# Where the silu's table is loaded, and five instructions or groups that change places in a decoder block kernel

## The reference, cut to what matters

```python
x = x + mamba2(layernorm(x), ...)       # state space layer, 128 heads of 64, 8 groups, state 128
x = x + cross_attention(layernorm(x), ctx, ctx, mask)   # 32 query heads, 8 key/value heads of 16
x = x + lora_experts(layernorm(x), A, B, Wr)            # 4 experts of rank 16, the best 2 by logits
```

```python
xBC = silu(conv4(proj_xBC) + conv_b)
dt = softplus(proj_dt + dt_bias)
y = ssd(x, A, B, C, D, dt)              # exp of differences of cumulated dt * A
g = y * silu(gate)
out = (g * rsqrt(mean(g * g, group) + eps) * norm_w) @ out_w.T
```

## Time and profile before

| what | us |
|---|---|
| median of 3 runs (3003.57 to 3009.27) | 3006.18 |
| the profiled execution's own time | 3005.64 |
| its span, first to last instruction | 3003.8 |
| PE busy (95% of the span) | 2865.4 |
| DVE busy (69%) | 2059.7 |
| ACT busy (48%) | 1437.4 |
| POOL busy (43%) | 1277.4 |
| ACT table loads, 183 of 1.28 us | 234.8 |

### The profile page before, as it was taken

How to read it: one execution, slowest core, us unless ns; L and a number is a source line. 1 busy time by engine, 2 the same in 40 slices (tenths; PEclk the granted TensorE clock), 3 DMA queues, 4 the chain that set the end, 5 groups by cost and what they waited for, 6 DMA issues and landing times.

```text
span 3003.8 us, 56158 instructions
## 1 busy us (share of the span) xinstructions
PE 2865.4 (95%) x22224; PEld 2294.5 (76%) x22224; DVE 2059.7 (69%) x3144; ACT 1437.4 (48%) x2077; POOL 1277.4 (43%) x820
## 2 busy tenths in 40 slices
PE   5899999999999999999999999999999999999986
PEld 3677777777878778787787878777787887878764
DVE  5677766777766767677676776777666676766656
ACT  3555556555444544444444454444444444444422
POOL 3566665666343343434334333424333342433332
PEclk8999999999999999999999999999999999999996
DMA  5777777777656655555655655555665555565510
GB/s 179 245 261 251 251 255 241 271 247 241 219 185 191 191 172 178 186 176 184 195 186 180 199 180 175 183 184 175 186 196 182 179 182 187 176 195 178 181 57 18
DMA packets 179266, 578.25 MB, mean 193 GB/s; under 512 B 25216, under 2 KB 31872, under 8 KB 170816
## 3 DMA queue, kind: packets, MB, share of 16 engines
q1 hardware_dynamic: 179008, 574.66, 58.5%
HBM read 460.29 MB, written 114.29 MB: 191 GB/s over the span
## 4 chain that ended last, share of the span: by engine, by line
PE 79%; DVE 13%; ACT 4%; issue 3%; DMA 0%; POOL 0%; DVEq 0%; ACTq 0%; SPq 0%; POOLq 0%
PE p_in L429 45%; PE p_out L429 21%; PE p_y L429 8%; PE p_in L508 4%; DVE cv L1148 3%; DVE o_ring L1092 2%; DVE t_y L1184 1%; ACT cv L775 1%; DVE decay L1167 1%; PE p_y L608 1%; DVE decay L1161 1%; ACT decay L775 1%; ACT L775 1%; ACT w_ring L775 0%; DVE x_tok L1172 0%
## 5 line engine op out<-in xcount | busy, mean ns | idle before, releaser
L429 PE MATMUL p_in<-xnb,w_ring 128*128 128x512 f32 x6912 | 1710.2, 400 | 24.1 <-DVE cv L1148 20.0
L429 PEld LDWEIGHTS p_in<-xnb,w_ring 128*128 128x128 f32 x6912 | 1281.3, 190 | 299.4 <-issue 24.1
L1148 DVE SCALAR_TENSOR_TENSOR cv<-p_in,cpar,cv 128x504 f32<-128x504 f32 (+2 forms) x960 | 704.5, 734 | 541.3 <-ACT cv L775 517.5
L1480 POOL TENSOR_TENSOR g_lo<-g_f,g_hi 128x512 fp32r<-128x512 f32 x256 | 332.1, 1297 | 1357.6 <-ACT g_hi L775 1357.6
L429 PE MATMUL p_out<-o_ring,g_hi 128*128 128x512 f32 x2048 | 648.8, 398 | 1.5 <-POOL g_lo L1480 1.5
L775 ACT ACTIVATE cv<-p_in,cpar 128x512 f32<-128x512 f32 x320 | 248.0, 775 | 703.5 <-PE p_in L429 622.5
L429 PEld LDWEIGHTS p_out<-o_ring,g_hi 128*128 128x128 f32 x2048 | 379.3, 188 | 89.7 <-issue 1.9
L429 PE MATMUL p_out<-o_ring,g_lo 128*128 128x512 f32 x1024 | 404.5, 395 | 0.0
L1172 DVE TENSOR_TENSOR x_tok<-p_in,dts 128x512 f32<-128x512 f32 x256 | 176.5, 689 | 289.1 <-PE p_in L508 288.0
L1491 POOL TENSOR_TENSOR ss<-ss,g_sq 128x512 f32<-128x512 f32 x192 | 309.6, 1612 | 7.5
L775 ACT ACTIVATE x_t<-cv 128x512 f32<-128x512 f32 x256 | 160.7, 628 | 302.1 <-DVE t_y L1184 287.0
(11 more groups left out here) (233 smaller groups left out, 2261.2 us busy)
## 6 DMA issues: line engine op xcount, KB each, us to landing
w_ring<-ws_scr SPq DMA_DIRECT2D x432, 512.0 KB, 3.6
o_ring<-ows_scr SPq DMA_DIRECT2D x192, 512.0 KB, 5.3
ws_scr<-w_ring SPq DMA_DIRECT2D x144, 512.0 KB, 4.9
decay<-cum_scr SPq DMA_DIRECT2D x128, 512.0 KB, 6.6
raw_w<-wt SPq DMA_DIRECT2D x144, 256.0 KB, 4.1
ows_scr<-o_ring SPq DMA_DIRECT2D x64, 512.0 KB, 6.2
raw_o<-owt SPq DMA_DIRECT2D x64, 256.5 KB, 5.7
acb<-x SPq DMA_DIRECT2D x3, 1024.0 KB, 6.4
```

The source lines that it names most:

```text
L429: return nc.tensor.matmul(o, lhsT=l, rhs=r, start=first, stop=last)
L1148: ins = V.scalar_tensor_tensor(acc[:, :, t:SEQ], src[:, :, 0:SEQ - t], cpar[:, 5 * m + 3 - t:5 * m + 4 - t], acc[:, :, t:SEQ], ALU.mult, A ...
L1480: T(g_lo[:, c % 2, :], g_f[:, c % 2, :], g_hi[:, c % 2, :].bitcast(F32), ALU.subtract).then_inc(glo_done, 1)
```

## The change

ScalarE gets a silu of one column into a spare tile, called at the start of each pass and at those steps that follow an exp, always directly behind `tap0`. On DVE `experts` moves from `early` to `late`, behind `scored`; the parts of the softplus get other steps; and `refill_o` of step 3 moves behind `late`. On GpSimd `deviation` moves behind `differences` of step 1 (and so behind `shifted`).

```diff
@@ scalar
+            def silu_table():
+                copy(spare[:, :], half_neg[:, 0:1], ACT.Silu)
@@
                 tap0(0, n)
+                silu_table()
                 silu(0, n)
@@
                 for k in range(1, CPG):
                     tap0(2 + k, n)
+                    if (k == 2 and (closing(tb, g) is not None or not begun)) or k == 3 or (k == 4 and is_at(tb, g, 4)) \
+                            or (k == 5 and former(opening(tb, g)) is not None):
+                        silu_table()
@@ vector, early
-                if k == 5 and former(t) is not None:
-                    experts(t - 1, S)
@@ vector, late
                 if k in (5, 6) and t is not None:
                     scored(t, S, k - 5, (y0, y1))
+                if k == 5 and former(t) is not None:
+                    experts(t - 1, S)
                 if k == 6 and u is not None:
                     attended(u, S, y0)
-                if is_at(tb, g, 4) and k in (6, 7):
-                    softplus(tb + 1, {6: (0,), 7: (1, 2)}[k])
-                if is_at(tb, g, 5) and k in (3, 6, 7):
-                    softplus(tb + 1, {3: (3,), 6: (4, 5), 7: (6, 7, 8, 9)}[k])
-                if is_at(tb, g, 6) and k in (3, 6, 7):
-                    softplus(tb + 1, {3: (10, 11), 6: (12,), 7: (13,)}[k])
+                if is_at(tb, g, 4) and k in (4, 7):
+                    softplus(tb + 1, {4: (0,), 7: (1,)}[k])
+                if is_at(tb, g, 5) and k in (3, 4, 6, 7):
+                    softplus(tb + 1, {3: (2,), 4: (3,), 6: (4, 5), 7: (6, 7)}[k])
+                if is_at(tb, g, 6) and k in (3, 4, 6, 7):
+                    softplus(tb + 1, {3: (8, 9), 4: (10,), 6: (11,), 7: (12, 13)}[k])
@@ vector, body
                     x_tokens(k, n)
-                    refill_o(k)
+                    if k != 3:
+                        refill_o(k)
@@
                     late(k, tb, g)
+                    if k == 3:
+                        refill_o(k)
@@ gpsimd, body
-                if coming(tb, g) is not None:
-                    deviation(coming(tb, g))
                 if u is not None:
                     shifted(u, S)
                 for k in range(1, CPG):
@@
                         differences(tb, g, 1, n)
+                        if coming(tb, g) is not None:
+                            deviation(coming(tb, g))
```

More of the change, by code:

```diff
@@ L113, in decoder_kernel @@
         rstd = sb("rstd", [P, 1])
+        spare = sb("spare", [P, 1])
         wd = sb("wd", [P, 2, KT, P], F32R)
```

## The result

The changed kernel takes 2981.55 us (median of 4 runs, 2979.32 to 2982.28), the kernel before 3007.43 beside it: ratio 0.9914, 95% interval 0.9897 to 0.9932. It was forecast at 2980.0 with a range of 2971 to 2994. The profiled execution took 2982.17 us with a span of 2980.4; before, 3005.64 and 3003.8. The total is 1.5 us off. Its parts are further off: two terms were wrong by 2 to 7 us each, in opposite directions.

The account below looks back on a forecast made before the run. TensorE bounds the kernel, so only ending its waits pays. Terms 13.5 + 0.3 + 7.4 + 3.3 + 4.4 + 0.5 - 3.0 - 0.4 = 26.0 us, taking the median 3006.2 to 2980; range 2971 to 2994.

Parts of the forecast that it names:

- The bound: Whole kernel: TensorE has the most work, so an edit pays only where it ends a TensorE wait, no more than that.
- The silu's table: Step 2 of odd passes, blocks 1 to 3: table load runs in ScalarE's idle 3.17 us, 13.5 us gained.
- Rival 2: Table load doesn't move, because the silu lands behind the wait or the load stays: 13.5 us less gain, 2994, chance 0.05.
- The output halves: Block 0, passes 0 to 3, step 3: low half begins earlier, head products' waits of 7.6 us go, 7.4 taken.
- The expert gates: Step 5 of passes 4 and 6: gates moved behind the scores end four waits, 4.1 us, 3.3 after 0.8 back.
- The softplus: Parts respread in blocks 0 to 2: block 0 gains 4.4 us; blocks 1 and 2 lose 0 to 1 each.
- Part 3 at step 4 of pass 5: Softplus part moved there in block 0 runs beside GpSimd's sums and costs perhaps 0.3 us.
- The deviation: Subtraction put ahead of it on GpSimd: costs 3.0 us in block 0's passes 1 to 3, 0.4 in blocks 1 and 2.
- both cases: Block 0, passes 1 to 3: `normal` ends 0.35 us later if first at the port, 1.3 if blocked for a `w_low`.
- The first pass: Subtractions start about 3 us earlier; TensorE's wait for the first decay matrix shrinks 0 to 1.9 us, 0.5 taken.
- Rival 4: Slower: `normal` is late by the whole subtraction, 3.69 us, in all passes: 3013, chance 0.04.
- Rivals 1 and 3: 1: block 0 gives its gains back, 2993, chance 0.14. 3: waits go whole and the deviation costs nothing, 2973, chance 0.09.

Follow-up runs that it names:

- the two runs: One-column silus alone on the kernel before: 2986.73 us, 18.9 less; changed kernel without the silus: 2999.05 us, 17.5 above the changed kernel.
- the old spread of the softplus: Changed kernel with the softplus parts at their old steps: 2982.24 us, ratio 0.9921; also with deviation behind the subtraction only in the first pass: 2976.39 us, 0.9897.
- two pairs: Changed kernel against two kernels with softplus at its old steps: one otherwise unchanged, 2982.24 us; one with deviation also ahead again except in the first pass, 2976.39 us.
- the hold: Changed kernel, with GpSimd in passes 1 to 3 of block 0 waiting until normal is done before its next w_low: 2978.25 us (one run).
- a second 91: Changed kernel with two one-column silus at each of the 91 places: 2981.41 us, ratio 0.9915.

## Why the prediction was right in sum, by its own steps

- **The bound.** Right: what paid was each wait of TensorE. Blocks 1 to 3 follow the sites to a tenth of a microsecond.
- **The silu's table.** The mechanism was right and the term, 13.5, too small: 15.3 us in the 12 odd passes (1.28 each by the 11 periods), 1.3 in pass 4 of blocks 1 and 2, 17.5 to 18.9 us in all by the two runs (block 0's dips and the tail in them). The step that failed is "Ten of the waits are 1.09 us and go whole": they do go whole, but it read the gain off the wait shown, 1.09, instead of the load removed from the chain, 1.28. No extra cost from 91 silus, as said. Rival 2 (the load doesn't move) is refuted by the load's place. On the drain the Trainium skill ("ScalarE: Activation LUTs", "What ACT_TABLE_LOAD costs") has about 2.66 us for each switch; by it the two waits of 1.65 us would have gone whole. They keep 0.37, so 1.28 us went, the load alone, and the one-column silu starts 0.01 us behind the load. No drain is seen here.
- **The output halves.** Right: 7.6 to 0.3 us of waits, 7.4 forecast; by periods up to 10, with clock dips in them.
- **The expert gates.** The wait of 4.1 us went, but not all of it by this edit alone: 1.2 us go with the silu at step 4 as well, and in pass 6 the edit is worth 3.1 us with the old spread of the softplus and 1.5 with the new one.
- **The softplus.** Wrong in sign: +4.4 forecast, -0.6 to -2.5 by the periods of two pairs. In block 0 the steps into passes 5 and 6 are as said: passes 4 and 5 gained 2.25 and 2.09 (1.77 and 1.9 forecast). But pass 6 lost 1.8 to 3.3, with and without a clock dip on the other side, where it was to gain 0.75 (2.0 - 1.25): the wait at step 4 fell by 1.65, the wait into pass 7 grew by 2.0, and a new wait of 1.29 us for x_t came at step 7. And blocks 1 and 2 lost 2.0 each in pass 5. The failed step is "Part 3 at step 4 of pass 5 runs beside GpSimd's sums, and costs perhaps 0.3", read together with "In blocks 1 and 2 nothing of it was waited for": there part 3 runs beside the subtraction too and takes 5.4 us more of Vector time, and TensorE waits 1.8 us. In block 0 the step was sound: part 3 takes 2.1 us more and still pays. Part 11 at step 6 of pass 6 was overlooked in the same way, and there block 0 loses. In block 0 after:

```profile
660.87 1.35 DVE L1123 SCALAR_TENSOR_TENSOR cum<-cum,d_s 128x512 f32<-128x512 f32 x1
662.25 1.41 DVE L1124 TENSOR_SCALAR dtraw<-dtraw 128x512 f32<-128x512 f32 x1
663.69 1.67 DVE L1125 SCALAR_TENSOR_TENSOR d_s<-cum,dtraw 128x512 f32<-128x512 f32 x1
665.40 1.40 DVE L1126 TENSOR_SCALAR d_s<-d_s 128x512 f32<-128x512 f32 x1
```

  5.9 us for four instructions that take 0.69, 0.43, 0.69 and 0.43 us where GpSimd is idle. All the evidence was at hand: the earlier trace rows show an instruction of 0.17 us taking 3.56 beside a subtraction. The prediction used it for the gates and not for the parts it moved. The Trainium skill ("SBUF — State Buffer", "Who interferes with whom") has the rule: a Vector instruction with two inputs from SBUF contends with GpSimd's reads, and a copy or scaling in its two-port mode with GpSimd for a whole instruction. Instructions with two inputs and scalings are in parts 3 and 11, and the rows agree.
- **The deviation.** The place and the sign were right. 3.0 us were taken, 3.7 measured, inside the range of 0.35 to 1.6 each, and both cases that the prediction worked out are there: 1.25 us late when `normal` is blocked for one `w_low` (1.3 forecast), 0.35 when it isn't, in passes 2 and 3 with the hold. It loses each time, as the rule of the Trainium skill ("SBUF — State Buffer", "Who interferes with whom") says, though the 4.8 worked out from it was too much. The first pass gave 1.1 in place of 0.5, and blocks 1 and 2 nothing in place of -0.4. Rival 4 fell: no further pass is late.
- **The sum.** The errors are +2 to +5 (silu), -5.0 to -6.9 (softplus), -0.7, +0.6 and +0.4 (deviation), and in block 0 some us of the clock and of the output halves' surplus. That they cancel is luck. That the time came out at 2981.55 says little for the parts; only taking them apart did. Rivals 1 and 3 fell too: block 0 kept 9.4 us, and the step 2 waits grew.

## What to carry to other kernels

An ACTIVATE of one column, placed where ScalarE waits anyway, moves a table load off the critical chain. Where TensorE waited for that chain it was worth up to the whole load (12 of the 91 sites here); at the 75 sites where nobody waited it was worth nothing. Before small Vector instructions are moved into a "free" step, look at what GpSimd runs in that step: beside a GpSimd instruction of 3.7 to 4.1 us a scaling of 0.43 us, a polynomial step of 0.69 and a 128x16 product of 0.17 all lasted until it ended (3.80, 4.19 and 3.56 us). And look at every block in which the step runs: what pays in one can cost in another. Where several edits are made at once, compare the periods of a repeated unit and not only the waits: they show each edit at its own place, and what two edits remove in common.

## What the runs showed of the hardware

- A blocked scaling of 128x512 on the Vector engine ended 0.28 to 0.29 us behind GpSimd's instruction: 166.89 behind 166.60, and 1265.06 behind 1264.78. In the earlier trace rows it was 0.28 too. The polynomial step with two inputs ended 0.55 us behind it (1307.43 behind 1306.88).
- 91 silus of one column, 0.20 us each, cost nothing that a second 91 would show, and the load takes 1.283 us at each of its 183 places, whatever stands before it.
- TensorE's granted clock fell to 0.50 in or behind some waits of 1.8 to 8.9 us in block 0, 6 to 10 times in 727 us, each time for 1.7 us of lost full-clock time; a mean of 0.99 hides it.
- The idle time shown ahead of a matmul was about 0.18 us less than what its removal gave, wherever a wait of 1.09 us went whole (1.24 to 1.30 us gained).
- The same code varied by up to 1.2 us in single passes of block 0, and by 3.4 us in the tail (183.5 to 186.9); in blocks 1 to 3 it repeats to 0.1 us but for single cases of 0.3.
